# A spiking-attention and mixture-of-experts layer in 32 overlapped chunks: the order of the last six beats is rearranged

## The reference

```python
# attention half: all scans run over the 512 steps
R, K, V = x @ Wr.T, x @ Wk.T, x @ Wv.T
# lif: v += (x_t - v)/2; s = v >= 1; v = 0 where s
h_t = 0.9 * h_(t-1) + lif(K)_t * lif(V)_t
x1  = layernorm(x + (lif(R)_t * h_t) @ Wo.T) * g1 + b1
s1  = lif(x1 @ W1.T + b1_)                 # 1024 wide
ffn = lif(s1 @ W2.T + b2_)
x2  = layernorm(x1 + ffn) * g2 + b2
x3  = layernorm(x + x2)
# expert half: 8 experts, the best 2 of a softmax gate
top, idx = top_k(softmax(x3 @ Wg + bg), 2); top /= sum(top)
out = layernorm(x3 + sum_k top[k] * (x3 @ We[idx[k]] + be[idx[k]]))
```

## Time and profile before

| | |
|---|---|
| timed runs | 1010.68, 1012.58, 1007.40 us |
| the profiled execution | 1007.83 us, of it a span of 1005.7 us |
| PE busy | 936.9 us, 93% of the span |
| VectorE busy | 909.4 us, 90% |
| ScalarE busy | 590.2 us, 59% |
| GpSimd busy | 560.5 us, 56% |
| mean granted TensorE clock | 0.974 of 2.4 GHz |
| the drain, beats 33 to 38 | from about 910.7 us to the end at 1005.7 us |

### The profile page before, as it was taken

One profiled execution on the slowest core, in us unless ns is written; L12 is line 12 of the kernel. 1 busy time (PEld: TensorE's weight loads), 2 busy tenths in 40 slices (PEclk: granted clock), 3 DMA queues, 4 the chain that ended last, 5 costly groups with the idle time before them and its releaser, 6 DMA issues.

```text
span 1005.7 us, 20280 instructions
## 1 busy us (share of the span) xinstructions
PE 936.9 (93%) x6400; PEld 865.5 (86%) x6400; DVE 909.4 (90%) x3669; ACT 590.2 (59%) x1352; POOL 560.5 (56%) x719
## 2 busy tenths in 40 slices
PE   5678788999999999999999999999999999999975
PEld 5577787999999999999999999999999999887764
DVE  4799988999999999999999999999999999998875
ACT  4455446665656666656666766656566666555452
POOL 0100213567776666676766666677766666674551
PEclk8789889999999999999999999999999999999998
DMA  5422222565554466555554555555544655545663
GB/s 170 121 69 66 40 53 53 108 124 109 110 108 96 105 122 121 117 116 106 108 109 100 116 117 119 122 116 104 107 99 103 127 116 106 105 95 112 134 129 78
DMA packets 57707, 106.53 MB, mean 106 GB/s; under 512 B 6400, under 2 KB 6400, under 8 KB 57600
## 3 DMA queue, kind: packets, MB, share of 16 engines
q0 software_dynamic: 36000, 65.55, 38.4%
q1 hardware_dynamic: 16992, 31.30, 9.7%
q10 hardware_dynamic: 4608, 8.39, 2.2%
HBM read 31.29 MB, written 8.39 MB: 39 GB/s over the span
## 4 chain that ended last, share of the span: by engine, by line
PE 76%; DVE 13%; ACT 4%; issue 3%; DMA 2%; POOL 2%; POOLq 0%; DVEq 0%; ACTq 0%
PE ps_e L362 29%; PE ps_proj L362 11%; PE ps_proj L427 11%; PE ps_proj L442 10%; PE ps_proj L448 5%; PE ps_attn L398 4%; DVE V L792 2%; DVE U L785 2%; PE ps_zx L406 2%; PE ps_attn L406 2%; DVE stats L864 1%; DMA xb<-x_tok 1%; DVE h L834 1%; ACT x_hi L610 1%; DVE s L1152 1%
## 5 line engine op out<-in xcount | busy, mean ns | idle before, releaser
L785 DVE SCALAR_TENSOR_TENSOR U<-V,U 128x256 f32<-128x256 f32 (+4 forms) x576 | 233.6, 406 | 5.5 <-ACT U L592 4.2
L1204 POOL TENSOR_SCALAR veps<-mv 128x2 f32<-128x2 f32 x128 | 47.1, 368 | 337.2 <-DVE mv L870 335.0
L362 PE MATMUL ps_e<-we_hi,x_hi 128*128 128x512 f32 (+2 forms) x640 | 229.2, 358 | 5.2 <-ACT term L631 3.3
L792 DVE SCALAR_TENSOR_TENSOR V<-U 128x256 f32<-128x256 f32 (+4 forms) x576 | 225.4, 391 | 1.5
L362 PE MATMUL ps_e<-we_lo,x_hi 128*128 128x512 f32 (+2 forms) x640 | 224.0, 350 | 0.0
L362 PE MATMUL ps_e<-we_hi,x_lo 128*128 128x512 f32 (+2 forms) x640 | 223.2, 349 | 0.0
L1218 POOL TENSOR_SCALAR s<-U 128x256 fp32r<-128x256 f32 x208 | 191.5, 955 | 15.7 <-DVE V L792 15.7
L631 ACT ACTIVATE term<-ps_e,gate 128x256 f32<-128x256 f32 x372 | 160.2, 474 | 49.5 <-PE ps_e L362 49.5
L592 ACT ACTIVATE U<-ps_proj,cst 128x256 f32<-128x256 f32 x320 | 135.0, 480 | 85.2 <-PE ps_proj L448 68.7
L577 ACT ACTIVATE U<-ps_proj 128x512 f32<-128x512 f32 x96 | 57.5, 599 | 151.9 <-PE ps_proj L362 151.9
L362 PEld LDWEIGHTS ps_e<-we_hi,x_hi 128*128 128x128 f32 x640 | 120.7, 189 | 19.3 <-ACT term L631 4.2
(11 more groups left out here) (89 smaller groups left out, 2210.5 us busy)
## 6 DMA issues: line engine op xcount, KB each, us to landing
acc<-term POOLq DMA_DIRECT2D x93, 256.0 KB, 3.4
...
```

Of the source, the lines that this page charges most:

```text
L362: mm = pe.matmul(dst, lhs, rhs, start=(i == 0), stop=(i == n - 1))
L785: v.scalar_tensor_tensor(out=U[:, s, t, c0:c1], in0=V[:, c0:c1], scalar=0.5, in1=U[:, s, t, c0:c1], op0=ALU.mult, op1=ALU.add).then_inc(do ...
L792: v.scalar_tensor_tensor(out=V[:, c0:c1], in0=u, scalar=THRESHOLD, in1=u, op0=ALU.is_lt, op1=ALU.mult).then_inc(done, 1)
L1204: g.tensor_scalar(veps[ln][:], mv[ln][:, :, 1], EPS, None, ALU.add).then_inc(rstd_ready[ln], 1)
```

## The change

It touches beats 33 to 38 only.

1. `expert0` of the next beat is issued ahead of `biases`, so ahead of the beat's end (beats 33 to 36).
2. `x3_T` comes after fill 4 instead of after fill 3, and ScalarE's copy of it after its read of fill 4.
3. The bias product goes to `ps_attn` instead of `ps_zx`. So `biases` no longer waits for x3's low half, `z_T` waits for `x3_lo_ready` instead of for `fin_sum` (in the beats after 33), and `gates_T`, which writes `ps_attn`, waits for `fin_sum`.
4. `fin_sum` moves from slot -1 to slot 8 (beats 34 to 37), so behind the gate and ahead of `ln2_add`. It stays in slot -1 in beat 33.
5. GpSimd issues `add_bias` ahead of the even and odd transfers of a beat (beats 33 to 36).
6. The last chunk's sum and result stand in `x1n`, which is free by then, instead of `res`. The wait for the store of `res` goes, and the last `bn_aggr` waits for `res_ready` of the chunk before.

```diff
-DRAIN = dict(z_sum=-1, y=(-1,) * 5, spikes_h1=-1, fin_sum=-1,
+DRAIN = dict(z_sum=-1, y=(-1,) * 5, spikes_h1=-1, fin_sum=8,
...
+        def bias_bank(k):
+
+            return ps_attn if Beat(k).late else ps_zx
+
+        def res_of(b):
+
+            return x1n if b.k == LAST_BEAT else res
...
                 pe.wait_ge(gate_steps, b.value(GATE_STEPS, LAG_M, GATE_STEPS))
+                if Beat(b.k - 1).late:
+                    pe.wait_ge(fin_steps, b.value(FIN_STEPS, LAG_F, 1))
...
-                if b.has(LAG_Z):
+                if b.has(LAG_Z) and not b.late:
                     pe.wait_ge(x3_lo_ready, b.value(1, LAG_Z, 1))
...
-                    mm = pe.matmul(ps_zx[:, j, :], gate_T[:, j, :], bias_stack[:], start=True, stop=True)
+                    mm = pe.matmul(bias_bank(b.k)[:, j, :], gate_T[:, j, :], bias_stack[:], start=True, stop=True)
...
                 pe.wait_ge(z_ready, b.value(2, LAG_Z, 2))
-                if b.has(LAG_F):
+                if Beat(b.k - 1).late:
+                    pe.wait_ge(x3_lo_ready, b.value(1, LAG_Z))
+                elif b.has(LAG_F):
                     pe.wait_ge(fin_steps, b.value(FIN_STEPS, LAG_F, 1))
...
-                if b.has(LAG_M) and b.k > LAG_M:
+                if b.has(LAG_M) and b.k > LAG_M and not Beat(b.k - 1).late:
                     expert0(b)
...
-                if b.has(LAG_Z) and not b.early:
+                if b.has(LAG_Z) and not b.early and not b.late:
                     x3_T(b)
...
                         expert(b, part)
+                        if part == 4 and b.has(LAG_Z) and b.late:
+                            x3_T(b)
+                    if b.late and not b.last_m:
+                        expert0(Beat(b.k + 1))
                     if not b.last_m:
                         biases(b)
...
                         read_expert(b, part)
+                        if part == 4 and b.has(LAG_Z) and b.late:
+                            read_x3(b)
...
-                    dve.wait_ge(out_stored, b.value(16, LAG_F))
-                    v.tensor_tensor(res[:], acc[:, b.slot(LAG_F, 2)], ps_zx[:], ALU.add).then_inc(fin_steps, 2)
+                    v.tensor_tensor(res_of(b)[:], acc[:, b.slot(LAG_F, 2)], bias_bank(b.k - 1)[:], ALU.add).then_inc(fin_steps, 2)
...
                 if step == 3:
+                    if b.k == LAST_BEAT:
+                        dve.wait_ge(res_ready, b.value(1, LAG_F))
...
-                if b.has(LAG_F) and slot == at["fin_sum"]:
+                if b.has(LAG_F) and slot == (at["fin_sum"] if not b.late or Beat(b.k - 1).late else -1):
                     fin_stage(b, 0)
...
+                if has_z and b.late:
+                    add_bias(b)
                 if sums:
                     add_even(b, LAG_F, 4)
                     add_odd(b, LAG_F, 5)
-                if has_z:
+                if has_z and not b.late:
                     add_bias(b)
```

11 lines of the change are left out of this document (7 added, 4 removed).

## The result

The kernel after took 1006.01 us (median of 14 runs, 1002.58 to 1007.43), the kernel before 1010.10 us on the same chip (14 runs, 1007.40 to 1012.58). The ratio is 0.9956, 95% interval 0.9943 to 0.9968, so the gain is about 4.4 us, where 6.85 us were summed. The forecast of 1002.4 us was 3.6 us too low; the time lies inside the range of 998.8 to 1007.3 us, at its upper end.

A forecast was written before the change was run, and what follows sets the result against it. With PE 93% and VectorE 90% busy, little short of less work would help; the change targeted waits in the last 95 us. Terms summed to -6.85 us, from the middle 1009.3 to 1002.4 us, range 998.8 to 1007.3.

The forecast's parts named there:

- Beat 33, `xb`, -1.13: Beat 33: with `add_bias` issued first, VectorE's wait for `xb` goes whole, a gain of 1.13 us.
- Beat 34, W2 behind the spikes, -1.06: Beat 34: with `fin_sum` out of the way, z's transposes need only z and W2 follows the spikes, gaining 1.06 us.
- x3's transposes, -2.67: Beats 34 to 36: x3's transposes one fill later, so all three PE waits ahead of them go, gaining 2.67 us.
- the biases, -0.72: Beats 34 to 36: biases behind `expert0` hide in PE's idle time before the gate, gaining 3 x 0.24 = 0.72 us.
- I take no new wait: Ahead of `expert0`, beats 34 to 36: x3's low half comes in time; other bound up to 0.5 us a beat.
- I am wrong if a wait stands ahead of `expert0` in any beat after 34: Sign that would refute the prediction: PE waiting ahead of `expert0` in a beat after 34.
- rival C: Beats 35 and 36: odd experts' transfers become the bound, losing 1.3 and 1.9 us; gain 3.6, 1005.7 us; chance 0.18.
- 14.2 us [...] It fits by 0.2: Beats 35 and 36: one chunk's chained odd transfers take 14.2 us, fitting new beats of 15.0 and 14.4 us.
- Expert 4's transfer is pushed back by one issue: Beat 33, `add_bias` first: expert 4's transfer up to 1.2 us later, delaying only the next even transfer, no engine.
- Rival B: Beat 34: idle PE's clock falls ahead of W2, losing 1.7 us; gain 5.15, 1004.2 us; chance 0.22.
- Beat 37, +0.6 for `fin_sum`: Beat 37: `fin_sum` lies between the gate and the sums fill 2 waits for, costing 0.6 us.
- The last sum, -1.97: End of the kernel: last chunk's sum in `x1n` no longer waits for the store of `res`, gaining 1.97 us.

The follow-up runs named there:

- version 5: Kernel after with `fin_sum` back in slot -1 in beats 34 to 37, the bias product staying in `ps_attn`; 1004.70 us, 0.9929 of before.
- version 10: Kernel after with `fin_sum` in slot -1, beat 36's biases ahead of `expert0`, and unread filler matmuls on PE in beats 34 to 37; 1002.16 us, 0.9905 of before.
- version 8: Kernel after with second norm's 1/std ahead of expert 6's transfer, PE fillers in beats 34 and 37, `fin_sum` in slot -1 in beat 37; 1003.29 us, 0.9917.
- version 6: Kernel after with `fin_sum` back in slot -1 in beat 37 alone; 1005.78 us, 0.9941 of before.
- version 4: Kernel after with unread filler matmuls on PE, 10 ahead of W2 in beat 34 and 16 ahead of fill 2 in beat 37; 1004.64 us, 0.9949 of before.
- Version 3: Kernel after with the second norm's 1/std ahead of expert 6's transfer on GpSimd, in the drain alone; 1004.79 us, 0.9944 of before.
- version 7: Kernel before with only part 5 of the change, `add_bias` issued first in the drain; 1008.31 us, 0.9978 of before.
- version 12: version 10 with the second norm's 1/std ahead of expert 6's transfer on GpSimd; 1003.25 us, 0.9947 of before.
- 2: Kernel after without part 5, `add_bias` back behind the first even and odd transfers; 1007.33 us, 0.9977 of before.
- 9: Kernel after with `fin_sum` in slot -1 in beats 34 to 37 and beat 36's biases ahead of `expert0`; 1003.21 us, 0.9922 of before.
- version 1: Kernel before with only part 6 of the change, the last chunk's sum in `x1n`; 1008.13 us, 0.9996 of before.

## Why the prediction was right or wrong

**Beat 33, `xb`, -1.13: right.** The wait is gone, and beat 33 lasts 17.27 us where 17.3 were worked out. Alone the part moved W2 of beat 34 by 1.44 us.

**Beat 34, W2 behind the spikes, -1.06: right in size, wrong in its cause.** With the term before it, 2.19 us were summed to W2, and 23.87 - 21.44 = 2.43 came. But I gave it to `fin_sum` "out of the way"; version 5 has it back in slot -1 and W2 starts as early. It was the bias product's new bank, which took `fin_sum` out of what z's transposes wait for.

**x3's transposes, -2.67, and the biases, -0.72: the waits went, the gain came in part.** The waits and the place of the biases are as forecast, and each beat reaches its sum somewhere: beat 35 is 15.08 us in version 10 (15.0 summed), beat 36 14.52 us in version 5 (14.4). But no version has both. Beats 35 and 36 together were summed at 29.4 us; before has 31.94, after 32.53, and the shortest are 30.66 (version 8, with a fall in beat 35) and 30.85 (version 10, without one). A beat 36 near its sum always followed a beat 35 that was longer. So of this part's 2.5 us in the two beats 1.2 came in no version. The next two steps say why.

**"I take no new wait", ahead of `expert0`: wrong in beat 36,** by 0.79 us (0.17 us in version 6, whose program is the same up to there; none in version 4). By the prediction's own sign, "I am wrong if a wait stands ahead of `expert0` in any beat after 34", its mechanism failed here. This is rival C, and the step that failed is its chain "14.2 us [...] It fits by 0.2". From VectorE's sum at 939.89 to the one at 958.06 the chain took 18.17 us: sum to expert 3's issue 3.69 (2.87 in the working), 3 to 5 3.90 (3.93), 5 to 7 6.61 (3.93), 7 to the sum 3.97 (3.5). The third link was priced as "the same" as the second, by a landing of its usual length, and three things stand in it. Expert 5's landing is itself longer (4.1 us here, 4.7 and 5.3 in version 10). Behind it GpSimd still has expert 6's transfer and the second norm's 1/std to do, until 952.65. Then expert 7's transfer waited for `fin_sum` in slot 8, until 953.50. With `fin_sum` early the link is still 5.37 us (version 5) and 5.44 us (version 10) in that beat; so slot 8 costs about 1.2 us of the 2.7, and the rest was to be seen in the trace of before:

```profile
949.52 0.86 POOL L1248 DMA_DIRECT2D odd_sum<-term  x1 [2.06 <-ACT term L631]
...
954.78 0.93 POOL L1248 DMA_DIRECT2D odd_sum<-term  x1
```

These are experts 5 and 7, 5.26 us apart. Version 5 shows what the slot does: with that one edit the waits for `odd_sum` and the one ahead of `expert0` of beat 36 are gone. The chain stays. In version 10 it takes 15.99 us from sum to sum, where 14.2 were worked out and the beat was to last 14.4: it doesn't fit, and the chance of 0.18 for rival C was too low.

**The same step left out GpSimd's queue.** That cost more: 2.01 us ahead of the gate's transposes of beat 36. "Expert 4's transfer is pushed back by one issue [...] and what waits for it is the next even transfer, no engine": the next even transfer is an instruction on GpSimd, and the 1/std of the second norm stands behind it on that engine. For beat 36 I had counted the `xb` wait as 1.1 us gained; it turned into 2.45 us. Version 3 shows the queue as the cause, version 7 that the new order of issue alone brings only 0.3 us of wait, and version 12 that the opposite order has its own price.

**Rival B happened**, with its price: half clock under W2 of beat 34, 1.6 us by version 4 (1.7 in the working), and the pauses ahead of it were those named. By the rule of the Trainium skill, TensorE: Matmul & The Clock Gate, "Part 1: The HAM clock gate (the "warmup" mystery)", half rate is the default, which activity releases, and the traces agree: no pause that had fillers was followed by a fall. Its chance of 0.22 was too low for the trace that was taken, but it isn't certain either: of the six profiled versions with that order ahead of W2 and no fillers (after, 2, 3, 5, 6, 9) two fell there. A fall is also not always lost whole: between versions 9 and 10 two falls went, worth 3.4 us, and the drain gained 1.63. What I didn't see is that the other pauses of about 2 us can bring one too: beat 35 did in five versions, beat 37 in five.

**Beat 37, +0.6 for `fin_sum`: right,** for what follows the gate: in version 3 VectorE's first addition starts 4.68 us from `expert0`, in version 1 4.08. In the kernel after fill 2 starts 6.76 us from `expert0`, 0.47 later than before, with a wait of 2.13 us and not of 2.5. In version 3 0.6 us more came behind it, as `odd_sum` was late for the sum there, too. **The last sum, -1.97: right** (1.78 in version 1). After has 24.20 us instead of 22.6 with a fall and no wait for `odd_sum` in that beat; version 4 has no fall, but a wait of 0.96 us for `odd_sum`, and 23.65 us.

**The whole.** The terms at both ends of the drain were right, and 5.7 us of waits and clock weren't in the sum in the profiled execution; about 2.4 us of them show in the medians. The timed runs' clocks are on record only as a mean over the whole span, so how often each fall comes in them isn't shown. That the time lies inside the range is in part luck: rivals B and C came together, with a wait that no rival named, and in the profile together they took 5.7 us, where B was priced at 1.7 and C at 3.2. The prediction took 5.05 us, 0.5%, for the least gain that can be told from none and gave 0.60 to a larger one; the gain is 4.4 us, and the interval still leaves out no change. Version 10, with `fin_sum` early, the clock held and the queue left as it is, gives 0.9905, 9.6 us of 1010.8. Its drain of 89.02 us is 0.8 us above the 88.2 summed, but 1.8 above the 87.2 expected of it.
